# Diagonal score blocks in strips of 64 queries, two groups in 17 chunks, one bound per branch

## The chip, the cores and the metric

The kernel runs on one core of one Trainium2 chip. The metric is the device time of one execution in microseconds; three runs of the kernel before gave 198.6 to 199.15 us, median 198.92 us.

## The reference

The input x has 1024 tokens of 256 numbers. It is layer-normed, goes through a causal attention with 16 heads and through a gated FFN, and both results are added to it.

```python
xn = layernorm(x)
q1, k1, q2, k2, v = split(xn @ Wqkv)          # 16 heads; q, k of 8 numbers each, v of 16
A1 = causal_softmax(q1 k1^T / sqrt(8)) v      # first branch
A2 = causal_softmax(q2 k2^T / sqrt(8)) v      # second branch
diff = (A1 - lam * A2) / rms * (1 - LAMBDA_INIT)
ffn = (gelu(fp8(xn) @ fp8(w_gating[0])) * (fp8(xn) @ fp8(w_gating[1]))) @ fp8(w_linear)
out = x + diff @ Wproj + ffn
```

## The kernel before

Tokens come in eight blocks (TB) of 128, P = 128. A group g is four heads (J) of one branch; there are eight groups, four (HG) for each branch, of which the first four are branch one. The queries and keys of a head lie in 32 rows of `q_st` and `k_st` (float32r, high and low parts stacked, so that a head's rows are 32j to 32j+31), the values in `v_all` (float32, 32 columns for a head: 16 values, a one in column 16, zeros behind).

Scores stand with keys on partitions and queries on columns. Of a group only blocks on or below the diagonal are made: 9 chunks of 512 columns per head, listed in `CHUNKS` (line 46) as (key block, blocks of queries, first query). Three of the nine have two pieces, (128, 384), (256, 256) and (128, 384) columns; eight 128-wide blocks on the diagonal are in five of them (`DIAGONALS`, line 51). A chunk of one head is an item and fills one PSUM bank; a unit is three items. A group is 36 items or 12 units (STEPS), the kernel 96 units (UNITS).

The main loop is `attention` (line 958). For each unit n TensorE runs
- `scores(n)` (line 877): it waits until exp n-2 is done (banks 0 to 2 and 3 to 5 take turns), then makes the pieces in rounds, the first piece of all three items, then the second. Each matmul has 32 rows of contraction, so the three heads sit in different row groups of the array. Its line in the profile is L898.
- `values_due(n)` (line 950): the probabilities of an earlier chunk times `v_all`, summed in bank 6; per piece one matmul for each of the four heads, in four column groups of 32 (`product`, line 906, profile line L910; float32, so each shows as two passes). They come 5 units after the chunk's last unit, 2 to 4 near the end (`due`, line 86).
- `beside(n)` (line 817): at hand-set units (V_AT, QK_AT, NORM_AT, DOWN_AT, lines 70 to 78) a part of the remaining projections of v, q and k (L758, L752), norms, or of the FFN's down product (L851). Some of these parts are split over two units.

ScalarE runs one exp of 1536 columns per unit (L442), from PSUM to one of six chunk slots of `probs`; its bias is a bound per group (`shift`, made by `bound`, line 454, once per branch). GpSimd zeroes the upper triangles of the diagonal blocks with one affine_select per chunk that has some (`mask`, line 356, L366), and has four squarings (L340) and four residual additions (L372) placed between masks. VectorE transposes each half of a group's sums out of bank 6 (`take`, L594), divides, subtracts the branches, normalizes and transposes back; it also takes the split projections and norms.

Ahead of the loop lie the input DMAs (x in four DMAs of two blocks: two on SyncE, L244, two on ScalarE, L385), the layer norm, transposes, first projections and the FFN's up product. Behind it lie the last output projections (`ending`, line 977) and five output DMAs (L312, L314, L452). Each output DMA holds 128 partitions, by whole blocks. On SP the output DMAs stand in one queue in the order of blocks 0-1, 2-3, 4-5, 7.

Of the kernel before, what the change touches and what calls it, by code (L numbers as in the profile page):

```python
# [15 lines left out]
P = 128  # L16
T = 1024
# [14 lines left out]
VW = 32  # L32
# [15 lines left out]
DIAGONALS = {0: [0], 1: [0, 128], 2: [0, 256], 4: [0], 6: [0, 128]}  # L48
NC = len(CHUNKS)
ITEMS = NC * J  # L50
PER_UNIT = 3
STEPS = ITEMS // PER_UNIT
UNITS = GROUPS * STEPS
BRANCH = HG * STEPS
KEPT = 6
STACKS = 4
MIXED, LAST = 2, 8
# [9 lines left out]
Y_BANK = (7, 7, 0, 0, 1, 2, 3, 4)  # L67
# [8 lines left out]
NORM_AT = {23: 0, 31: 1, 39: 2, 41: 3}  # L76
DOWN_AT = {44: (0, 0, 4), 45: (0, 4, 8), 49: (1, 0, 8), 56: (2, 0, 4), 57: (2, 4, 8), 61: (3, 0, 8), 65: (4, 0, 8),
           68: (5, 0, 4), 69: (5, 4, 8), 73: (6, 0, 8), 79: (7, 0, 4), 80: (7, 4, 8)}


def last_unit(chunk):

    return (chunk * J + J - 1) // PER_UNIT


def due(g, c):

    if g < GROUPS - 2:
        late = 5
    elif g < GROUPS - 1:  # L90
        late = 4
    else:
        late = (3, 3, 3, 3, 3, 2, 2, 2, 2)[c]
    return g * STEPS + last_unit(c) + late


def diagonals_until(g, c):

    return g * len(DIAGONALS) + sorted(DIAGONALS).index(c) + 1

# [19 lines left out]
def diff_attention_ffn_kernel(nc, x, w_qkv, w_proj, lq1, lk1, lq2, lk2, w_gating, w_linear, out):  # L120
    x_rows = x[0].rearrange("(b p) c -> p b c", p=P)
    out_rows = out[0].rearrange("(b p) c -> p b c", p=P)

    with ExitStack() as ctx:
# [31 lines left out]
        max_rest = arena[0:HG * J, 3 * T:5 * T].rearrange("p (a t) -> p a t", a=2)  # L156
        max_junk = arena[:, 5 * T:6 * T].bitcast(BF16).rearrange("p (a t) -> p a t", a=2)
# [6 lines left out]
        w_q = sb("w_q", [P, KC, 3 * C], F32)  # L164
        causal = sb("causal", [P, T], BF16)

        o_t = sb("o_t", [P, 2, 16, VW], F32)
        attn1 = sb("attn1", [P, HG, 32, DV], F32)

        squares = sb("squares", [P, 4, T], BF16)  # L170
# [868 lines left out]
```

## Time and profile before

| | us | |
|---|---|---|
| median of three runs | 198.92 | 198.6 to 199.15 |
| the profiled execution | 199.27 | its span 197.5 |
| TensorE matmul busy | 182.2 | 92% of the span |
| ScalarE busy | 163.6 | 83% |
| VectorE busy | 92.4 | 47% |
| GpSimd busy | 59.4 | 30% |
| mean granted TensorE clock | 0.993 | |

The span runs from the first to the last instruction; 1.8 us of the profiled execution lie outside it. Matmuls overlap in the array, so that the busy time of TensorE counts a stretch as busy when any matmul is in flight. The chain of waits is the sequence of work, followed back from the last instruction, in which each piece was what the next one waited for or ran behind. Its pieces for one stretch, listed in order of time, lie end to end, so the length of a piece is what it costs on that path.

### The profile page before, as it was taken

To read this page: it belongs to the slowest core of one execution; us is meant where nothing else is said; L and a number is where in the kernel's file an instruction comes from. 1 tells how busy PE (TensorE), PEld (TensorE's weight loads), DVE (VectorE), ACT (ScalarE), POOL (GpSimd) and SP (SyncE) were. 2 spreads that over 40 slices of the span, in tenths; PEclk is the share of its full clock that TensorE was granted. 3 is DMA by queue.
4 is the path that set the end of the run, shared out by engine and by line. 5 is a ranking of instruction groups with operands and counts; after the bars stand their busy time and mean duration, and the time that the engine had idled before them with its cause. 6 is when DMAs were issued, how large, how long until landed. Compare 5 with 4: busy or idle time off the path is not lost.

```text
span 197.5 us, 3554 instructions
## 1 busy us (share of the span) xinstructions
PE 182.2 (92%) x1446; PEld 78.3 (40%) x1450; DVE 92.4 (47%) x218; ACT 163.6 (83%) x136; POOL 59.4 (30%) x71
## 2 busy tenths in 40 slices
PE   6899989899999999999989999999998999899940
PEld 6855334454332323242333424344342423233830
DVE  0975798431223240540472025216703697895840
ACT  2156865899999999999999999999999899998010
POOL 8526600042216142314442043235216124320000
PEclk9999999999999999999999999999999999999997
DMA  5967377780000000000277781000000000000051
GB/s 174 404 242 245 73 179 205 207 190 10 0 0 3 0 0 3 0 0 3 60 203 188 181 191 39 0 3 0 0 3 0 0 3 0 0 3 0 0 178 44
DMA packets 8149, 14.99 MB, mean 76 GB/s; under 512 B 1984, under 2 KB 5312, under 8 KB 8128
## 3 DMA queue, kind: packets, MB, share of 16 engines
q1 hardware_dynamic: 7440, 14.05, 25.5%
q10 hardware_dynamic: 688, 0.66, 1.0%
q8 instruction: 14, 0.23, 0.5%
q14 instruction: 7, 0.06, 0.1%
HBM read 5.26 MB, written 1.05 MB: 32 GB/s over the span
## 4 chain that ended last, share of the span: by engine, by line
PE 74%; ACT 15%; DVE 4%; POOL 1%; issue 1%; POOLq 0%; DVEq 0%
PE ps L910 29%; PE ps L898 17%; ACT probs L442 13%; PE ps L752 8%; PE ps L758 4%; PE ps L941 4%; PE ps L747 3%; PE ps L851 3%; PE ps L813 3%; DVE area L529 2%; DVE o_t L594 1%; ACT probs L430 1%; PE ps L742 1%; PE ps L947 1%; ACT L430 1%
## 5 line engine op out<-in xcount | busy, mean ns | idle before, releaser
L442 ACT ACTIVATE probs<-ps,shift 128x1536 f32<-128x1536 f32 x96 | 140.1, 1554 | 2.4 <-PE ps L898 1.6
L910 PE MATMUL ps<-probs,v_all 128*32 128x512 f32 (+3 forms) x768 | 78.1, 496 | 1.5 <-DVE o_t L594 1.5
L366 POOL TENSOR_SCALAR_AFFINE_SELECT probs<-probs 128x1024 f32<-128x1024 f32 (+1 forms) x40 | 36.7, 917 | 109.7 <-ACT probs L442 109.6
L898 PE MATMUL ps<-q_st,k_st 32*128 32x512 f32 (+3 forms) x384 | 49.8, 420 | 1.2 <-issue 0.8
L898 PEld LDWEIGHTS ps<-q_st,k_st 32*128 32x128 f32 x384 | 22.4, 182 | 58.6 <-ACT probs L442 30.4
L594 DVE STREAM_TRANSPOSE o_t<-ps 128x512 f32<-128x512 f32 x16 | 11.5, 717 | 49.5 <-PE ps L910 49.5
L910 PEld LDWEIGHTS ps<-probs,v_all 128*32 128x32 f32 x768 | 16.4, 108 | 19.6 <-issue 13.9
L752 PE MATMUL ps<-xn_t,w_q 128*128 128x512 f32 (+1 forms) x38 | 17.3, 557 | 0.8 <-ACT xn_t L393 0.8
L813 PE MATMUL ps<-area 128*128 128x512 fp8e4 x64 | 14.5, 379 | 1.0 <-DVE area L529 1.0
L430 ACT ACTIVATE probs<-ps 128x512 bf16<-128x512 f32 x16 | 9.3, 597 | 4.5 <-PE ps L813 2.7
L529 DVE TENSOR_TENSOR area<-ps,probs 128x512 fp8e4<-128x512 f32 x16 | 10.5, 687 | 1.8 <-ACT probs L430 1.7
L813 PEld LDWEIGHTS ps<-area 128*128 128x128 fp8e4 x64 | 6.0, 97 | 9.5 <-issue 3.4
L758 PE MATMUL ps<-w_q,xn_t 128*128 128x256 f32 x32 | 8.7, 399 | 1.0 <-DVE area L529 1.0
L650 DVE CAST parts<-ps 128x512 fp32r<-128x512 f32 x4 | 2.8, 691 | 14.2 <-PE ps L752 14.1
L752 PEld LDWEIGHTS ps<-xn_t,w_q 128*128 128x128 f32 x38 | 6.2, 189 | 7.3 <-issue 7.0
L851 PE MATMUL ps<-area 128*128 128x256 fp8e4 x64 | 9.1, 275 | 0.0
L941 PE MATMUL ps<-w_p,squares 128*128 128x256 f32 x32 | 8.4, 389 | 0.0
L747 PE MATMUL ps<-ident 128*128 128x128 f32 x36 | 6.8, 378 | 1.6 <-POOL ident L321 1.6
L747 PEld LDWEIGHTS ps<-ident 128*128 128x128 f32 x36 | 6.6, 290 | 1.6 <-POOL ident L321 1.6
L496 DVE TENSOR_TENSOR parts<-ps,parts 128x512 fp32r<-128x512 f32 x8 | 5.5, 690 | 3.5 <-ACT parts L399 3.4
L851 PEld LDWEIGHTS ps<-area 128*128 128x128 fp8e4 x64 | 5.3, 97 | 4.6 <-issue 4.1
L941 PEld LDWEIGHTS ps<-w_p,squares 128*128 128x128 f32 x32 | 5.8, 190 | 2.6 <-issue 1.9
(78 smaller groups left out, 117.2 us busy)
## 6 DMA issues: line engine op xcount, KB each, us to landing
q_st<-parts SPq DMA_DIRECT2D x32, 128.0 KB, 2.8
k_st<-parts SPq DMA_DIRECT2D x32, 128.0 KB, 2.8
probs<-L_ffn_w_gating SPq DMA_DIRECT2D x4, 512.0 KB, 7.8
probs<-L_ffn_w_linear SPq DMA_DIRECT2D x1, 1024.0 KB, 13.1
w_q<-L_attn_Wqkv SPq DMA_DIRECT2D x2, 384.0 KB, 5.8
out<-probs SPq DMA_DIRECT2D x3, 256.0 KB, 3.0
x_sb<-L_attn_x SPq DMA_DIRECT2D x2, 256.0 KB, 4.2
x_sb<-L_attn_x ACTq DMA_DIRECT2D x2, 256.0 KB, 4.5
```

The costliest lines, as they stand in the source:

```text
L366: pool.affine_select(out=blocks, in_=blocks, pattern=pattern, compare_op=ALU.is_ge, fill=0.0, base=0, channel_multiplier=-1).then_inc(mask ...
L442: act.activation(probs[:, at:at + PER_UNIT, :].rearrange("p s u -> p (s u)"), ps[:, 3 * (n % 2):3 * (n % 2) + 3, :].rearrange("p b n -> p ...
L529: dve.tensor_tensor(hidden[:, c, h * HALF:(h + 1) * HALF], ps[:, 2 * PAIR[n] + 1, :], gated[:, n % RING, :], ALU.mult, saturate=False).the ...
L594: dve.transpose(o_t[:, h, :, :].rearrange("p b w -> p (b w)"), ps[:, 6, :]).then_inc(o_taken, 1)
L747: pe.matmul(ps[:, 7, 0:P], ident[:, :], ident[:, :], start=True, stop=True)
L752: return pe.matmul(ps[:, bank, at:at + wide], w_q[:, k, i * P:(i + 1) * P], xn_t[:, k, h * HALF + at:h * HALF + at + wide], start=(k == 0 ...
L758: ins = pe.matmul(ps[:, bank, (b % 2) * C:(b % 2 + 1) * C], xn_t[:, k, b * P:(b + 1) * P], w_q[:, k, 2 * C:3 * C], start=(k == 0), stop=(k ...
L813: ins = pe.matmul(ps[:, 2 * PAIR[n] + g, :], w_gate8[:, g, k, c * P:(c + 1) * P], x8[:, k, h * HALF:(h + 1) * HALF], start=(k == 0), stop= ...
L851: ins = pe.matmul(ps[:, 7, (b % 2) * C:(b % 2 + 1) * C], hidden[:, c, b * P:(b + 1) * P], w_lin8[:, c, :], start=(c == 0), stop=(c == HC - 1))
L898: ins = pe.matmul(ps[:, bank, at:at + wide * P], k_st[rows, g % STACKS, kb * P:(kb + 1) * P], q_st[rows, g % STACKS, queries], start=True, ...
L910: ins = pe.matmul(ps[32 * j:32 * j + 32, 6, q0 % HALF:q0 % HALF + wide * P], v_all[:, g % HG, kb, 32 * j:32 * j + 32], probs[:, slot + j, ...
L941: ins = pe.matmul(ps[:, Y_BANK[b], at:at + C], out_t[:, p, b * P:(b + 1) * P], w_p[:, p, :], start=(p == 0 and at == 0), stop=(p == 1), sk ...
```

## The change

- The two diagonal blocks of an even and the next odd key block (a and a+1) are made in 192 columns instead of 256. Halves of blocks change places: in every odd block the lower and the upper 64 tokens are exchanged. A strip of 64 queries then needs all 128 keys of its own block, or 64 keys of each of two blocks, stacked on the 128 partitions. For that `v_all` gets a second copy (EARLY) that holds zeros where the other block's keys lie.
- Four of 17 chunks of a pair of groups hold such diagonals: eight pieces of 64 columns and one of 128 each. Two pieces of four write a strip of the same 64 columns, the second of them over 64 partitions only, so that eight pieces cover 384 columns.
- Two groups share 17 chunks (before 2 times 9). The kernel has 272 items in 92 units: 89 of three items, two of two and one of one, the odd ones at the middle and the end (STARTS).
- Per chunk with diagonals there are two affine_selects of 64 partitions and 1024 elements; 16 such chunks in all.
- One bound per branch instead of one per group serves as bias of the exps.
- `v_all` has 17 columns per head (VW), not 32; VectorE makes the EARLY copies with four copies.
- Parts of `beside` that were split over two units are whole, and all of them have new units; squarings and residual additions have new places; the delay of the values (LATER) is 5 units, 6, 4, 3 or 2 for some chunks.
- Every DMA of x and of the output that had 128 partitions becomes two of 64 partitions.

```diff
+def diagonal(at, a, c):
+    b, d = a + 1, c + 1
+    return [(at, b, FULL, b * P, MINOR), (at + 64, d, FULL, d * P, MINOR),
+            (at + 128, b, EARLY, b * P + MINOR, MINOR), (at + 128, a, EARLY, a * P, MINOR),
+            (at + 192, d, EARLY, d * P + MINOR, MINOR), (at + 192, c, EARLY, c * P, MINOR),
+            (at + 256, a, FULL, a * P + MINOR, MINOR), (at + 320, c, FULL, c * P + MINOR, MINOR)]
 CHUNKS = [
-    [(0, 4, 0)], [(3, 1, 384), (1, 3, 128)], [(2, 2, 256), (6, 2, 768)], [(0, 4, 512)], [(4, 4, 512)],
-    [(1, 4, 512)], [(7, 1, 896), (5, 3, 640)], [(2, 4, 512)], [(3, 4, 512)],
+    [(0, 0, diagonal(0, 0, 2) + [(384, 2, FULL, 384, 128)])],
+    [(0, 0, [(0, 0, FULL, 128, 384), (384, 1, FULL, 256, 128)])],
+    [(0, 0, [(0, 1, FULL, 384, 128)]), (0, 1, [(128, 4, FULL, 640, 384)])],
...
 ]
+MASKED = (0, 7, 9, 11)
+STARTS = list(range(0, ITEMS // 2, 3)) + [ITEMS // 2] + list(range(ITEMS // 2 + 2, ITEMS, 3)) + [ITEMS]
-QK_AT = {8: (4, 0, 0, 256), 9: (4, 0, 256, 256), 13: (4, 1, 0, 512), 17: (5, 0, 0, 512), 20: (5, 1, 0, 256),
-         21: (5, 1, 256, 256), 25: (6, 0, 0, 512), 29: (6, 1, 0, 512), 32: (7, 0, 0, 256), 33: (7, 0, 256, 256),
-         37: (7, 1, 0, 512)}
+QK_AT = {8: (4, 0, 0, 512), 13: (4, 1, 0, 512), 21: (5, 0, 0, 512), 25: (5, 1, 0, 512), 29: (6, 0, 0, 512),
+         32: (6, 1, 0, 512), 37: (7, 0, 0, 512), 39: (7, 1, 0, 512)}
+NORM_AT = {17: 0, 28: 1, 35: 2, 42: 3}
+DOWN_AT = {47: (0, 0, 8), 50: (1, 0, 8), 54: (2, 0, 8), 58: (3, 0, 8), 62: (4, 0, 8), 66: (5, 0, 8), 70: (6, 0, 8),
+           74: (7, 0, 8)}
+LATER = {20: 6, 26: 6, **{k: 4 for k in range(57, 63)}, 63: 3, 64: 3, 65: 3, 66: 2, 67: 2}
...
-            for b in (0, 4):
-                sp.dma_start(x_sb[:, b:b + 2, :], x_rows[:, b:b + 2, :]).then_inc(x_in[b // 2], 16)
+            for i in (0, 2):
+                for p0, rows in halves:
+                    sp.dma_start(x_sb[p0:p0 + MINOR, 2 * i:2 * i + 2, :], x_rows[:, i, rows, :]).then_inc(x_in[i], 16)
...
+            def mask(k):
+                at = k % KEPT * J
+                pool.wait_ge(exp_done, last_unit(k) + 1)
+                for p0, first in ((0, 0), (MINOR, P)):
+                    strips = probs[p0:p0 + MINOR, at:at + J, first:first + 4 * MINOR].rearrange(
+                        "p j (s u) -> p j s u", s=4)
+                    pool.affine_select(out=strips, in_=strips, pattern=[[0, J], [0, 4], [1, MINOR]],
+                                       compare_op=ALU.is_ge, fill=0.0, base=0, channel_multiplier=-1
+                                       ).then_inc(masked, 1)
+                    pool.wait_ge(masked, masks_until(k) - (p0 == 0))
...
-                for p in range(2):
+                for p in range(max(len(h) for h in heads)):
+                    for h in heads:
+                        if p < len(h):
+                            ins = score(*h[p], general)
...
+            def score(g, j, bank, piece, general):
+                at, kb, part, q0, wide = piece
+                rows, queries = slice(32 * j, 32 * j + 32), slice(q0, q0 + wide)
+                keys = MINOR if part == EARLY and kb % 2 == 0 else P
+                out = ps[0:keys, bank, at:at + wide]
+                ins = pe.matmul(out, k_st[rows, g % STACKS, kb * P:kb * P + keys], q_st[rows, g % STACKS, queries],
+                                start=True, stop=not general)
...
+                for at, kb, of, q0, wide in pieces:
+                    for j in range(J):
+                        ins = pe.matmul(ps[32 * j:32 * j + VW, 6, q0 % HALF:q0 % HALF + wide],
+                                        v_all[:, of, g % HG, kb, VW * j:VW * j + VW], probs[:, slot + j, at:at + wide],
+                                        start=first, stop=False, skip_group_check=True)
+                    first = False
```

## Rows read from the trace of the kernel before

**Rows 1.** The page's busy time, share of the span and instructions of each engine.

```profile
PE 182.2 (92%) x1446; PEld 78.3 (40%) x1450; DVE 92.4 (47%) x218; ACT 163.6 (83%) x136; POOL 59.4 (30%) x71
```

**Rows 2.** Groups by line: busy us, mean ns of one, idle before.

```profile
L442 ACT ACTIVATE probs<-ps,shift 128x1536 f32<-128x1536 f32 x96 | 140.1, 1554 | 2.4 <-PE ps L898 1.6
L430 ACT ACTIVATE probs<-ps 128x512 bf16<-128x512 f32 x16 | 9.3, 597 | 4.5 <-PE ps L813 2.7 <-DVE area L529 1.8
L366 POOL TENSOR_SCALAR_AFFINE_SELECT probs<-probs 128x1024 f32<-128x1024 f32 (+1 forms) x40 | 36.7, 917 | 109.7 <-ACT probs L442 109.6
```

**Rows 3.** The chain of waits from 45 to 60 us: start, length, what.

```profile
45.02 1.06 PE ps L758 x4
46.08 0.43 PE ps L898 x2
46.50 1.00 PE ps L910 x8
47.50 0.43 PE ps L898 x2
47.93 1.00 PE ps L910 x16
48.93 0.48 PE ps L898 x5
49.41 0.57 PE ps L910 x8
49.98 0.63 PE ps L752 x2
50.61 0.48 PE ps L898 x3
51.09 0.57 PE ps L910 x8
51.66 0.63 PE ps L752 x2
...
56.58 0.48 PE ps L898 x4
57.06 1.05 PE ps L752 x2
```

**Rows 4.** The chain of waits from 117 to 131 us.

```profile
117.92 0.99 PE ps L910 x8
118.91 0.43 PE ps L898 x2
...
121.40 0.54 PE ps L851 x4
...
128.30 0.98 PE ps L851 x8
```

**Rows 5.** ScalarE's instructions from 120 to 139 us: start, length, what.

```profile
118.68 21.58 ACT L442 ACTIVATE probs<-ps,shift 128x1536 f32<-128x1536 f32 x15
```

**Rows 6.** TensorE's matmuls, then its weight loads, from 83.4 to 87.4 us.

```profile
83.49 0.50 PE L898 MATMUL ps<-q_st,k_st 32*128 32x512 f32 x3
83.93 1.07 PE L910 MATMUL ps<-probs,v_all 128*32 128x128 f32 x16
85.25 0.55 PE L898 MATMUL ps<-q_st,k_st 32*128 32x128 f32 x6 [0.25 <-issue]
85.73 0.64 PE L910 MATMUL ps<-probs,v_all 128*32 128x256 f32 x8
...
85.25 0.30 PEld L898 LDWEIGHTS ps<-q_st,k_st 32*128 32x128 f32 x6 [0.23 <-issue]
```

**Rows 7.** Weight loads of the two lines: duration ns least, median, most.

```profile
L898 PEld LDWEIGHTS ps<-q_st,k_st x384: 180/181/186, 35.9 to 178.4; 32*128 32x128 f32 x192
L910 PEld LDWEIGHTS ps<-probs,v_all x768: 105/109/111, 46.4 to 181.8; 128*32 128x32 f32 x192
```

**Rows 8.** The chain of waits from 1 to 21 us.

```profile
8.40 0.89 PE ps L742 x8
```

**Rows 9.** The start: queues and VectorE, start, length, what, idle before.

```profile
0.80 0.95 SPq L244 DMA_DIRECT2D x_sb<-L_attn_x  x2
4.53 1.41 DVE L475 BATCH_NORM_STATS2 stats<-x_sb 128x6 f32<-128x256 f32 x4 [4.53 <-DMA x_sb<-L_attn_x]
```

**Rows 10.** The end: SyncE's queue from 188 us on.

```profile
188.34 2.73 SPq L312 DMA_DIRECT2D out<-probs  x3
191.11 0.50 SPq L314 DMA_DIRECT2D out<-probs  x1
```

**Rows 11.** Who waited for whom: us in total, times, longest.

```profile
PEld ps L910 <- POOL probs L366: 2.2, 7, 0.8
PEld ps L910 <- DVE o_t L594: 2.1, 8, 0.8
```

More of the change, by code:

```diff
@@ L65, with unit_of, last_unit, due @@
 WARM_UP = 18
-Y_BANK = (7, 7, 0, 0, 1, 2, 3, 4)
+Y_BANK = (7, 7, 5, 5, 0, 1, 2, 3)
 V_AT = {0: (2,), 1: (3,), 2: (4,), 3: (5,), 4: (6,), 5: (7,)}
-QK_AT = {8: (4, 0, 0, 256), 9: (4, 0, 256, 256), 13: (4, 1, 0, 512), 17: (5, 0, 0, 512), 20: (5, 1, 0, 256),
-         21: (5, 1, 256, 256), 25: (6, 0, 0, 512), 29: (6, 1, 0, 512), 32: (7, 0, 0, 256), 33: (7, 0, 256, 256),
-         37: (7, 1, 0, 512)}
[L76 to L99, printed above, removed]
+QK_AT = {8: (4, 0, 0, 512), 13: (4, 1, 0, 512), 21: (5, 0, 0, 512), 25: (5, 1, 0, 512), 29: (6, 0, 0, 512),
[4 more added lines that the diff above has]
+LATER = {20: 6, 26: 6, **{k: 4 for k in range(57, 63)}, 63: 3, 64: 3, 65: 3, 66: 2, 67: 2}
+def unit_of(item):
+    return max(n for n in range(UNITS) if STARTS[n] <= item)
+def last_unit(k):
+    return unit_of(k * J + J - 1)
+def due(k):
+    return last_unit(k) + LATER.get(k, 5)
+def ends(g):
+    return last_unit(g // 2 * NC + (8, 16)[g % 2])
+def begins(g):
+    return unit_of((g // 2 * NC + (0, 8)[g % 2]) * J)
+def masks_until(k):
+    return 2 * (k // NC * len(MASKED) + MASKED.index(k % NC) + 1)
 class Own:
@@ L672, in _ @@
             keep(0, 1)
+            norm_round(0)
             keep(1, 0)
             split(5)
-            norm_round(0)
             keep(1, 1)
-            split(6)
             norm_round(1)
             keep(2, 0)
+            split(6)
+            norm_round(2)
+            take(2, 1)
             split(7)
-            norm_round(2)
-            keep(2, 1)
+            divide(2, 1)
+            take(3, 0)
             norm_round(3)
@@ L931, in second_half @@
-            def second_half(g):
-                first, (kb, wide, q0) = CHUNKS[MIXED]
-                pe.wait_ge(o_taken, 2 * g + 1)
-                product(g, MIXED, first[1] * P, kb, wide, q0, True)
+                heads = []
+                for e, item in enumerate(range(STARTS[n], STARTS[n + 1])):
+                    k, j = item // J, item % J
+                    heads.append([(2 * (k // NC) + gi, j, 3 * (n % 2) + e, piece)
+                                  for gi, _, pieces in CHUNKS[k % NC] for piece in pieces])
@@ new lines, in values @@
+            def values(k, part):
+                c, slot = k % NC, k % KEPT * J
+                gi, h, pieces = CHUNKS[c][part]
+                g = 2 * (k // NC) + gi
+                if c in MASKED:
+                    pe.wait_ge(masked, masks_until(k))
+                else:
+                    pe.wait_ge(exp_done, last_unit(k) + 1)
+                if k == 0:
+                    pe.wait_ge(v_ones, 1)
+                    pe.wait_ge(zeros_set, 1)
+                    pe.wait_ge(v_out, 6)
+                    pe.wait_ge(early_out, 2)
+                if k == 2 and part == 1:
+                    pe.wait_ge(v_out, TB)
+                if k == 7:
+                    pe.wait_ge(early_out, 4)
+                first = (c, part) in OPENS
+                if first and (g, h) != (0, 0):
+                    pe.wait_ge(o_taken, 2 * g + h)
+                for at, kb, of, q0, wide in pieces:
[4 more added lines that the diff above has]
+                    first = False
+                if (c, part) in CLOSES:
+                    ins.then_inc(o_ready, 1)
@@ L950, in values_due @@
             def values_due(n, first, end):
-                for g in range(first, end):
-                    for c in range(NC):
-                        if due(g, c) == n:
-                            values(g, c)
-                        if c == MIXED and due(g, c) + 1 == n:
-                            second_half(g)
+                for k in range(first, end):
+                    for part in range(len(CHUNKS[k % NC])):
+                        if due(k) + part == n:
+                            values(k, part)
             def attention(br, general):
```

231 lines of the change are left out of this document (112 added, 119 removed).

## The prediction

> **What bounds the kernel now.** I read the busy times first [rows 1]: TensorE 92%, ScalarE 83%, the others under half. That names two candidates and decides nothing, because matmuls in flight side by side make TensorE look busy. So I took the chain of waits for stretches of the main loop [rows 3, 4]. There the pieces lie end to end and all of them are TensorE's: one unit's scores last 0.43 us, the values of a chunk 0.99 to 1.00, a projection part 1.05, and the next scores start as the piece before ends. The scores take the time of their 512 columns whether one head or three run beside each other in their row groups. So a unit with a chunk of values costs TensorE 0.43 + 1.00 = 1.43 us.
>
> Then ScalarE. Fifteen exps in a row begin 118.68 and end 21.58 later [rows 5]; less the last one's own length, some 1.6, this is 14 distances in 20 us, 1.42 to 1.43 us each. ScalarE's step and TensorE's step are the same to a hundredth, so either may be the bound. What decides is who gives way: ScalarE lost only 2.4 us in the whole loop [rows 2], but it cannot start an exp before its scores are there, and where TensorE has a dearer unit (0.48 for scores with a first piece of 128 columns, 0.57 + 0.63 beside them [rows 3], 1.68 together) the step of the kernel is 1.68, not 1.43. I take the loop as bound by TensorE, with ScalarE close behind. The reader should carry this away: an engine that is released from work gains nothing here if TensorE gets more.
>
> **The change part by part.** The sum is made against the profiled execution, 199.27 us; the median is 0.35 below it.
>
> Exps. 288 items of 512 columns become 272, that is 89 exps of 1536 columns, two of 1024, one of 512. At 1.43 for 1536, and by proportion for the rest, ScalarE needs 127.3 + 1.9 + 0.5 = 129.7 instead of 96 x 1.43 = 137.3 us: 7.6 less. This is off the path if TensorE is the bound, and counts zero.
>
> Units. Four units fewer. Each costs a round of scores, 0.43, and the switch back from values, which is 1.00 less the two passes of 0.43 = 0.14, of which I count 0.11. 4 x 0.54 = -2.2 us.
>
> Columns. Scores and values keep theirs. Chunks with diagonals have 8 x 64 + 128 = 640 columns on TensorE though only 512 for ScalarE, since two strips are written and read twice: a pair of groups has 4 x 640 + 13 x 512 = 9216, exactly the 18 x 512 of before. So TensorE is relieved of no stream; the saving is ScalarE's alone.
>
> Small score pieces, the largest term. A chunk with diagonals runs nine rounds, eight of 64 columns. A stream of 64 columns is 0.43/8 = 0.053 us, but each piece needs the weights of another key block in the same row group. Their spacing shows in the unit at 85.25 [rows 6]: six weight loads in two rounds last from 85.25 over 0.30 us, a single one 0.18 [rows 7], so the second round's load begins about 0.11 after the first. Transposes with 128 columns of weights and 128 of stream run at 0.89/8 = 0.11 [rows 8]. I therefore take 0.107 for a round with 128 keys and, by half its columns, 0.053 for the two rounds with 64. Eight distances: 6 x 0.107 + 2 x 0.053 = 0.75; first piece with its extra 0.05 (the 0.48 of a 128-column start less 0.43); last piece of 128 columns, 0.107. Together 0.91 against 0.43: +0.48 us. Four items never fit a unit of three, so each of the 16 chunks touches two units, and in a mixed unit the other heads' pieces end long before the nine rounds do: 32 units x 0.48 = +15.4 us. The lower bound is stream alone, 9 rounds in 0.53: +0.10 each, +3.3 us. The upper is the only distance from a short round to the next that the trace has: 0.48 less 384 columns at 0.32 is 0.16. 8 x 0.16 + 0.11 = 1.39, +0.96 each, +30.7 us. I choose 0.107, since loads were seen to follow each other at it.
>
> The units of before with a 128-column first piece, four per group, go: 32 x (0.48 - 0.43) = -1.6 us.
>
> Small value pieces. 16 chunks x 8 pieces x 2 passes = 256 passes of 64 columns. Two-piece chunks of before cost no more than single ones, 1.00 for sixteen matmuls against 1.00 for eight [rows 3], so a pass costs its stream and some nanoseconds: I take 3 ns, +0.8 us. Lower bound 0. The upper bound is one value weight load per pass, 0.109 [rows 7] instead of 0.053: +14 us. Seventeen instead of 32 columns of weights can only shorten the load; where it is hidden, this is nothing, and I count nothing.
>
> Joined parts. Three split projections, 2 x 0.63, become 1.05: -0.6. Four split down products, 2 x 0.54, become one of 0.98 [rows 4]: -0.4. Together -1.0 us.
>
> Masks. A mask of 1024 elements took about 1.1 (mean of both forms 0.92 [rows 2]); now two in a row for each chunk, 64 partitions each, with the same length: 2.3 us after the exp instead of 0.65 to 1.1. The total stays, 32 x 1.1 = 35 against 36.7. Values come five units after the chunk's last one; TensorE is at most two units ahead, so three steps, 4.3 us, cover 2.3, and also a residual of 1.2 ahead of it. With LATER 4 two steps, 2.9, cover 2.3 barely. Now the wait for masks is 2.2 us in total [rows 11], most of it hidden behind running matmuls. Zero, at most +2. What queues behind a late mask is TensorE's whole order.
>
> VectorE. Four more copies of some 0.5 us at a time when it is busy a quarter; shorter bound by one small reduction; zero. Its waits for TensorE around `take` remain; TensorE's waits for the transposes [rows 11] remain too, 16 halves as before.
>
> The odd units at the middle: ScalarE has 0.5 us of work where TensorE needs a whole round; TensorE does not wait for that. The flag of branch two comes from norms in unit 42 for unit 46, four steps, 5.7 us, for about 3 us of VectorE's work. Zero to +1.
>
> DMAs. An issue takes 0.5 us of a queue [rows 9, 10]. The first statistics wait for the first x, 4.53, and everything behind hangs on it; its second half is issued one place later: +0.4. w_q and the FFN's weights come 1 us later, which their users' 2 us of margin cover. At the end SyncE issues 8 instead of 4 DMAs, ScalarE 2 instead of 1; the last two wait for the same block, and the queue is full already (2.73 us for three). +0.5 at least, +1.7 if all of the queue's doubling shows; I take 1.0. Together +1.4 us.
>
> **Sum:** -2.2 + 15.4 - 1.6 + 0.8 - 1.0 + 1.4 = +12.8, so 199.27 + 12.8 = 212.1 us, 211.7 against the median; I say 212.
>
> **A rule of the pages.** The distance of 0.107 us for 128 columns of weights is what the trace gives in two places. The Trainium skill, "TensorE: Matmul & The Clock Gate", section "LDWEIGHTS (loading the stationary operand)", puts a load at its columns over 1.2 in ns, 107 for 128 and 53 for 64, whatever the rows; by that rule the sum stays as it is, and the trace agrees. It stands here because it denies the cheap case below: row groups don't make a load shorter.
>
> **The rivals.**
>
> *Small rounds cost their stream only.* For it: loads of other row groups start some ns apart [rows 6]. Against it: the 0.48 of a short first piece. The 15.4 becomes 3.3: 200.0 us.
>
> *ScalarE is the bound and the kernel gets faster.* The price of a diagonal unit would have to lie within what ScalarE's step leaves. Mixed units could hide the rounds beside other heads' 512 columns, and late scores be caught up by the two sets of banks. Then exps give -7.6, the DMAs +1.4: 193.1 us. For it: the steps are equal, 1.43, and ScalarE is never idle for long. Against it: in the chain of the loop nearly everything is TensorE, without a gap. It decides from an added TensorE time, small score and value pieces together, of under 2.2 + 1.6 + 1.0 - 1.4 = 3.4 us, which is 0.1 us per diagonal unit; above that the kernel is slower.
>
> *Every small round costs the long distance, or the array is emptied between tile shapes.* Rounds with 64 keys use another width of tile than those with 128, four changes in nine rounds. A change of shape is in the trace from values to scores, 0.11 to 0.14 us. Four of these per diagonal unit are +0.44 to 0.56, 32 x 0.5 = +16: 228 us. All rounds at 0.16 instead give +15.3 on the sum: 227.4 us. For it: 0.16 is the measured distance. Against it: the switch from scores to values costs nothing visible (0.43 for the scores before it). The Trainium skill, "TensorEngine Tiling (Array Packing)", section "Key Properties", says that changing the tiling mode drains the engine; by that rule this rival is the one that comes, and the 0.14 of the trace agrees in one direction of the two.
>
> *Every small value pass costs a whole weight load:* +13 on the sum, 225 us.
>
> **How the numbers follow.** Forecast, 207 to 218: 0.50. Cheap rounds, 198.5 to 206: 0.16. Long distance or emptied array, alone or in part, over 218 (224 to 229 in full): 0.18. Whole loads for value passes: 0.07. Faster, ScalarE bound: 0.09. The range takes the cheap rounds' 200 below and 228 above: 200 to 228. About 0.3% is what a measurement can tell from no change. Slower by over 0.3% hold the forecast, both dear cases and most of the cheap one: 0.87. Within 0.3%: 0.04, a part of the cheap case. Faster: 0.09.
>
> **What the new profile would show.** Scores of a unit with diagonals as chain pieces of about 0.9 us, eighteen or more matmuls each; 0.55 means the cheap case, 1.4 the dear one. Values of such a chunk about 1.05 to 1.1; 1.9 would be the load per pass. ScalarE with idle time ahead of exps, released by the scores, some 20 us in all, where it had 2.4; its step 1.43 in stretches without diagonals. TensorE's chain share up. First statistics at 4.9 to 5.0, and some 10 DMA issues at the end. What would make it wrong: exps still at 1.43 through the diagonal chunks, or TensorE waiting for masks for more than 2 us.

## The result and the profile after

Four runs of the changed kernel gave 223.03 to 229.54 us, median 224.8, beside 199.03 (198.6 to 199.22) for the kernel before: ratio 1.127, 95% interval 1.122 to 1.132. It is slower, and by about twice what the 212 of the prediction said. The profiled execution took 224.58 us (span 222.9) at a mean granted clock of 0.968, where before had 199.27 (197.5) at 0.993. Times and clock go together in the four runs (0.972 for the shortest, 0.952 for the longest); runs that the granted clock disturbed as a whole are left out of the ratios here and below.

First the page's busy times and the largest groups (columns as in [rows 1, 2]):

```profile
PE 202.4 (91%) x2879; PEld 113.3 (51%) x2884; DVE 97.4 (44%) x220; ACT 159.4 (72%) x132; POOL 60.0 (27%) x66
L505 ACT ACTIVATE probs<-ps,shift 128x1536 f32<-128x1536 f32 (+1 forms) x92 | 135.8, 1522 | 28.5 <-PE ps L979 27.8
L421 POOL TENSOR_SCALAR_AFFINE_SELECT probs<-probs 64x1024 f32<-64x1024 f32 x32 | 37.2, 1163 | 109.1 <-ACT probs L505 108.0
```

ScalarE's exps take 4.3 us less than in [rows 2], as the change wants, and ScalarE is idle ahead of them for 28.5 us where it was for 2.4; nearly all of that ended with scores (L979). TensorE has twice the instructions. The masks take as long in all as before, and no wait of TensorE for them is left. The shares of the chain of waits in the whole span, before and then after, show whose path grew:

```profile
PE 74%; ACT 15%; DVE 4%; POOL 1%; issue 1%; POOLq 0%; DVEq 0%
PE 72%; DVE 11%; DMA 4%; ACT 3%; issue 3%; SPq 2%; another core or an unknown queue 0%; DVEq 0%
```

The 15% of ScalarE before are in good part exps of the loop, 25.0 us, which the stretches of [rows 3, 4] do not hold. One piece of them:

```profile
110.07 7.30 ACT probs L442 x5
```

After the change nearly all of them are off the chain, and VectorE (DVE) stands there with 11% in place of 4%.

The chain of waits from 45 to 60 us, the same stretch as [rows 3]:

```profile
48.40 0.43 PE ps L979 x2
48.83 1.24 PE ps L1009 x72
...
55.13 1.04 PE ps L979 x20
56.17 0.98 PE ps L1009 x8
57.16 0.44 PE ps L979 x6
57.59 0.98 PE ps L1009 x8
58.58 1.04 PE ps L979 x27
```

Scores with nine rounds take 1.04 us whether all three heads have them (27 matmuls) or only some (20), against 0.43 for plain ones. The values of a chunk with diagonals (72 matmuls) take 1.24, of a plain one 0.98.

Start and end:

```profile
6.83 1.41 DVE L537 BATCH_NORM_STATS2 stats<-x_sb 128x6 f32<-128x256 f32 x4 [6.83 <-DMA x_sb<-L_attn_x]
213.36 5.81 SPq L362 DMA_DIRECT2D out<-probs  x6
219.22 1.80 SPq L365 DMA_DIRECT2D out<-probs  x2
```

Statistics start at 6.83 instead of 4.53 [rows 9]; eight output DMAs of 64 partitions hold SyncE's queue for 7.6 us, where four took 3.2 [rows 10]. From VectorE's last addition to the end of the span it is 7.5 us instead of 7.2.

The middle, in the chain from 108 to 132 us:

```profile
109.37 1.07 PE ps L827 x2
...
110.47 0.70 DVE parts L720
...
111.19 0.70 DVE parts L558
...
111.97 0.50 SPq L312
...
112.51 0.59 SPq L314
...
116.36 3.19 DMA k_st<-parts
...
119.60 1.62 PE ps L979 x18
121.22 1.84 PE ps L1009 x8
123.06 1.89 PE ps L979 x11
```

The last projection part (L827) is followed by VectorE's split, seven stacking DMAs issued one after another, and the landing of the last; the first scores of the second branch wait for it. Then the same pieces that took 1.04 and 0.98 take 1.9 and 1.84. The stretches of 5 us show why:

```profile
core 0: us, PE busy (x) PEld busy (x) DVE busy (x) ACT busy (x) POOL busy (x), PEclk, DMA share, GB/s
115.00:120.00 5.00, 3.82 (x107) 2.40 (x106) 2.71 (x13) 3.87 (x4) 0.00 (x0) 1.00 0.74 189
120.00:125.00 5.00, 5.00 (x48) 3.08 (x49) 0.00 (x0) 1.12 (x2) 0.00 (x0) 0.50 0.68 161
125.00:130.00 5.00, 5.00 (x26) 1.73 (x27) 0.00 (x0) 2.15 (x2) 2.30 (x2) 0.50 0.81 203
130.00:135.00 5.00, 4.59 (x64) 2.23 (x60) 1.40 (x3) 4.61 (x4) 0.00 (x0) 0.97 0.89 189
```

TensorE was idle for 1.2 of the 5 us before 120; from there it was granted 1.2 instead of 2.4 GHz for 10.2 us, which is 5.1 us of full speed.

**Where 25.3 us come from.** Ahead of the loop +1.7: the first exp begins at 39.73 instead of 38.01. In the loop, from the first exp to the start of the last, +22.2: 163.1 instead of 140.9. Behind it +1.4: 1.1 of that is one part of the output projection, which now stands behind the last exp and stood ahead of it, and 0.3 is the tail with the DMAs.

For the loop I count pieces at their price in the chain. Scores: before 96 x 0.43 + 32 x 0.05 = 42.9, after 32 x 1.04 + 60 x 0.43 = 59.1: +16.2. Values: before 72 x 0.995 = 71.6, after 16 x 1.24 + 52 x 0.98 = 70.8: -0.8. The half clock +5.1. TensorE's idle time in the loop is 7.75 us where it was 3.31, +4.4; in it are the wait for `k_st`, 0.9, and the waits for VectorE's transposes (`o_t`), 3.7 instead of 1.5. Joined parts by their lengths -1.0, and the projection part that left the loop -1.1. That is 22.8 where 22.2 were measured. It is a count times a price, not a sum of rows: in the chain of the kernel before, 25.0 of the loop's 140.9 us are exps, so that each term is known less well than the total suggests.

### The profile page after: what moved, and what is told of

The parts are those of the page before. It is cut to its first block, busy times and chain, and to the rows that moved or that the text cites. A ratio compares the mean times of both kernels' runs of the same rounds, so it can differ in the third digit from the quotient of the medians.

```text
span 222.9 us, 6456 instructions
## 1 busy us (share of the span) xinstructions
PE 202.4 (91%) x2879; PEld 113.3 (51%) x2884; DVE 97.4 (44%) x220; ACT 159.4 (72%) x132; POOL 60.0 (27%) x66
## 3 DMA queue, kind: packets, MB, share of 16 engines
HBM read 5.26 MB, written 1.05 MB: 28 GB/s over the span
## 4 chain that ended last, share of the span: by engine, by line
PE 72%; DVE 11%; DMA 4%; ACT 3%; issue 3%; SPq 2%; another core or an unknown queue 0%; DVEq 0%
PE ps L1009 27%; PE ps L979 23%; PE ps L827 7%; PE ps L833 4%; PE ps L922 3%; PE ps L1020 3%; PE ps L888 3%; DMA x_sb<-L_attn_x 2%; DVE o_t L656 2%; DVE area L591 2%; DMA k_st<-parts 1%; PE ps L817 1%; SPq L312 1%; ACT probs L493 1%; SPq L314 1%
## 5 line engine op out<-in xcount | busy, mean ns | idle before, releaser
L505 ACT ACTIVATE probs<-ps,shift 128x1536 f32<-128x1536 f32 (+1 forms) x92 | 135.8, 1522 | 28.5 <-PE ps L979 27.8
L1009 PE MATMUL ps<-probs,v_all 128*17 128x64 f32 (+4 forms) x1728 | 79.3, 315 | 4.2 <-DVE o_t L656 3.7
L979 PEld LDWEIGHTS ps<-q_st,k_st 32*128 32x128 f32 (+1 forms) x864 | 46.3, 182 | 48.6 <-issue 35.3
L979 PE MATMUL ps<-q_st,k_st 32*128 32x64 f32 (+5 forms) x864 | 67.6, 317 | 2.4 <-issue 1.0
L421 POOL TENSOR_SCALAR_AFFINE_SELECT probs<-probs 64x1024 f32<-64x1024 f32 x32 | 37.2, 1163 | 109.1 <-ACT probs L505 108.0
L1009 PEld LDWEIGHTS ps<-probs,v_all 128*17 128x17 f32 x1728 | 27.6, 97 | 21.2 <-issue 13.7
L827 PE MATMUL ps<-xn_t,w_q 128*128 128x512 f32 x32 | 16.4, 621 | 1.2 <-ACT xn_t L456 0.8
L888 PEld LDWEIGHTS ps<-area 128*128 128x128 fp8e4 x64 | 6.0, 97 | 9.3 <-issue 3.2
L827 PEld LDWEIGHTS ps<-xn_t,w_q 128*128 128x128 f32 x32 | 5.3, 189 | 6.2 <-issue 4.9
L922 PEld LDWEIGHTS ps<-area 128*128 128x128 fp8e4 x64 | 5.9, 103 | 4.6 <-issue 2.4
L392 POOL TENSOR_TENSOR squares<-parts 128x512 bf16<-128x512 f32 x4 | 4.2, 1042 | 12.8 <-DVE parts L720 12.2
```

Source lines behind the costliest of these rows:

```text
L421: pool.affine_select(out=strips, in_=strips, pattern=[[0, J], [0, 4], [1, MINOR]], compare_op=ALU.is_ge, fill=0.0, base=0, channel_multipl ...
L505: act.activation(probs[:, at:at + many, :].rearrange("p s u -> p (s u)"), ps[:, 3 * (n % 2):3 * (n % 2) + many, :].rearrange("p b n -> p ( ...
L827: return pe.matmul(ps[:, bank, at:at + wide], w_q[:, k, i * P:(i + 1) * P], xn_t[:, k, h * HALF + at:h * HALF + at + wide], start=(k == 0 ...
L888: ins = pe.matmul(ps[:, 2 * PAIR[n] + g, :], w_gate8[:, g, k, c * P:(c + 1) * P], x8[:, k, h * HALF:(h + 1) * HALF], start=(k == 0), stop= ...
L922: ins = pe.matmul(ps[:, 7, (b % 2) * C:(b % 2 + 1) * C], hidden[:, c, b * P:(b + 1) * P], w_lin8[:, c, :], start=(c == 0), stop=(c == HC - 1))
L979: ins = pe.matmul(out, k_st[rows, g % STACKS, kb * P:kb * P + keys], q_st[rows, g % STACKS, queries], start=True, stop=not general)
```

## The experiments

### The DMAs alone

```diff
-                sp.dma_start(x_sb[:, b:b + 2, :], x_rows[:, b:b + 2, :]).then_inc(x_in[b // 2], 16)
+                for p0 in (0, 64):
+                    sp.dma_start(x_sb[p0:p0 + 64, b:b + 2, :], x_rows[p0:p0 + 64, b:b + 2, :]).then_inc(x_in[b // 2], 16)
```

(the same for ScalarE's two, and for the five of the output)

> The kernel before, with each DMA of x and of the output as two of 64 partitions and nothing else. In the changed kernel a half DMA holds its queue for 0.6 to 0.8 us and the first statistics begin at 6.83 instead of 4.53 us, the first exp at 39.73 instead of 38.01, and from the last exp to the end it takes 20.0 instead of 18.6 us. Theory: all of that is the DMAs', so 199.0 + 1.7 + 1.5 = 202.2 us. Rival, as forecast: half a place in the queue at each end, 199.0 + 1.4 = 200.4 us.

Measured: 202.3 us, ratio 1.014 (1.010 to 1.018) to the kernel before. In SyncE's queue at the end:

```profile
191.26 4.74 SPq L314 DMA_DIRECT2D out<-probs  x6
196.05 2.97 SPq L317 DMA_DIRECT2D out<-probs  x2
```

A row's mean misleads here, since three of the rows hold one long issue each: 1.60 us in the row of three of [rows 10], 1.30 and 2.33 in these two. The others take 0.60 to 0.70 for 64 partitions and 0.42 to 0.50 for 128. At the start four take 2.99 in both kernels with halves, 0.75 each against 0.48 [rows 9]. So a half is dearer to issue than a whole.

The 2.9 us are not all of that, though. In the profiled run the first exp comes 2.9 us later than before, and 1.7 of these are the clock:

```profile
10.00:15.00 5.00, 4.22 (x9) 1.88 (x8) 3.98 (x15) 1.39 (x4) 0.00 (x0) 0.66 0.99 375
```

The first projections, 3.67 us in the kernel before and in the changed one, take 5.37 here. TensorE had waited 1.8 and 0.8 us ahead of them. Without the clock the halves cost 1.2 at the start and 0.4 behind the last exp, 1.6 in all; the run of the four with the highest mean clock, 0.990, took 201.15, 1.8 above before. Then the lower halves of x went on SyncE's queue and the upper ones on ScalarE's:

```diff
-            for b in (0, 4):
-                for p0 in (0, 64):
-                    sp.dma_start(x_sb[p0:p0 + 64, ...
+            for b in (0, 2, 4, 6):
+                sp.dma_start(x_sb[0:64, b:b + 2, :], x_rows[0:64, b:b + 2, :]).then_inc(x_in[b // 2], 16)
```

> e1, with the lower halves of x on SyncE's queue and the upper ones on ScalarE's, so that both halves of the first two blocks are first in their queues. Theory: e1's loss at the start is the second half's place behind a first of 0.75 us; the first exp comes some 1.2 us earlier than in e1 and the time is 202.3 - 1.2 = 201.1 us. Rival: half DMAs are slower in themselves, 202.3 us.

Measured: 200.65 us, ratio 1.0075 (1.0045 to 1.0105). 2.9 us above before have become 1.5. The order in the queue does what was expected for the first statistics, which start at 4.00 us (before 4.53, with the halves in one queue 6.05). But the profiled run (203.1 us) has its first exp at 40.89, no earlier than that kernel's 40.87: its first projections wait for `w_q` until 11.15, whose issues now stand behind four of x, and then take 5.40 at half clock. The faster runs have a mean clock of 0.988 to 0.990. How much of the 1.4 us is order and how much is clock is not shown.

### The small score pieces

Here the diagonal chunks' scores are made in two pieces of 384 and 128 columns; the exchange of halves is not computed, so part of the scores is left out.

```diff
-                                  for gi, _, pieces in CHUNKS[k % NC] for piece in pieces])
+                                  for gi, _, pieces in CHUNKS[k % NC] for piece in one_piece(k % NC, pieces)])
```

> The changed kernel, where the eight small score pieces of a diagonal chunk are one of 384 columns with one key block; the scores are not those of the reference. Theory: a unit with diagonals takes 0.44 instead of 1.04 us on TensorE and all of it is on the path: 224.8 - 32 x 0.60 = 205.6 us. Rival: TensorE's rounds are partly hidden and ScalarE or the half clock takes over, under half of it comes back: over 215 us.

Measured: 209.9 us, ratio 1.051 (1.048 to 1.055): 14.9 less than the changed kernel, the largest single part. The chain shows 0.43 where 1.04 was, that is 32 x 0.61 = 19.5 less; some 4 of it came back as a wait, of value matmuls for VectorE's transposes of the sums (who waited for whom, TensorE):

```profile
PE ps L1016 <- DVE o_t L663: 7.8, 10, 3.4
```

In the changed kernel the same row says 3.7 us, 7 times. The next kernel keeps the nine rounds and gives each of the eight small ones 64 keys (half of the keys of six rounds is left out):

```diff
-                keys = MINOR if part == EARLY and kb % 2 == 0 else P
+                keys = MINOR if wide == MINOR else P
```

> The changed kernel, where all eight small score pieces load 64 keys instead of six with 128 and two with 64, so that half of each block's keys is left out. The streams are unchanged. Theory: the columns of the weight load pace a round, 0.111 us for 128 and 0.057 for 64: six rounds 0.054 shorter, a unit with diagonals 0.72 instead of 1.04 us, 224.8 - 32 x 0.32 = 214.5 us. Rival, tile shapes that differ cost a drain and loads cost nothing: rounds of one shape save only the four changes, and those took nothing in the trace, so 224.8 us.

Measured: 213.86 us, ratio 1.078 (1.071 to 1.085): 10.9 less. The unit with 27 matmuls, first in the changed kernel, then here (timeline, weight loads: start, length):

```profile
58.51 0.97 PEld L979 LDWEIGHTS ps<-q_st,k_st 32*128 32x128 f32 x27 [0.85 <-ACT probs L505]
```

```profile
56.99 0.65 PEld L979 LDWEIGHTS ps<-q_st,k_st 32*64 32x64 f32 x27 [0.85 <-ACT probs L505]
57.06 0.72 PE ps L979 x27
```

Columns streamed and the number of matmuls are the same, only the key columns of six rounds are halved, and the loads shrink by 0.32. The first row less a single load's 0.18 [rows 7] is 0.79 for eight distances, six with 128 keys and two with 64. One by one, the loads of a round begin 0.109 to 0.112 us behind those of the round before if that had 128 keys, and 0.059 if it had 64 (0.055 to 0.059 in the second kernel). Six times 0.053 less is the 0.32. The spacing of rounds is the weight load. It also denies the emptied array: the changed kernel has four changes between 64 and 128 keys in a unit, this one only that to the last piece, and there is nothing left over for changes beyond those six halves. The rule of the Trainium skill, "TensorEngine Tiling (Array Packing)", section "Key Properties", that a change of the tiling mode drains the engine, finds no cost at this change of width.

The total fits less well than it seems: 10.9 measured for 32 x 0.32 = 10.2, but the profiled run of this kernel has no half clock in the loop, where the changed kernel lost 5.1, so that the agreement of the totals is in part chance.

Last, two pieces of an odd block made by one matmul that streams 128 columns into both strips, with the projections placed earlier (as in the experiments on the middle, below).

```diff
+                if wide == BOTH:
+                    out = ps[:, bank, 0:4 * MINOR].rearrange("p (s e u) -> p s e u", s=2, e=2)[:, :, at // MINOR, :]
```

> e2, with the two score pieces of each odd block made by one matmul of 128 columns into two strips: seven rounds instead of nine, result unchanged. Theory: two loads of 128 columns fewer per unit with diagonals, 32 x 0.22 = 7.0 us under e2's 221.6: 214.6 us. Rival: the streams are what counts, and those are the same: 221.6 us.

Measured: 212.95 us, ratio 1.070 (1.068 to 1.073). Two rounds fewer per unit give 0.82 in place of 1.04:

```profile
58.10 0.82 PE ps L996 x19
```

32 x 0.22 = 7.0, and 8.6 were gained on the kernel that it was made from, whose profiled run lost 1.7 in the loop to half clock where this one lost nothing; 7.0 + 1.7 is 8.7. Still 14 us short of the kernel before.

### The small value pieces

```diff
-                for at, kb, of, q0, wide in pieces:
+                for at, kb, of, q0, wide in one_piece(c, pieces):
```

Part of the values' sums is left out by this.

> The changed kernel, where the eight small value pieces of a diagonal chunk are one of 384 columns with one set of values; the sums are not those of the reference. Theory: a diagonal chunk's values take 0.98 instead of 1.24 us: 224.8 - 16 x 0.26 = 220.6 us. Rival: the rest of the chain hides them, 224 us or more.

Measured: 222.63 us, ratio 1.114 (1.107 to 1.120), 2.2 less. Its runs spread over 4 us and the changed kernel's over 6.5, so the direction fits and the size stays open; the 1.24 and 0.98 of the chain are the better number: 16 x 0.26 = 4.2 for the diagonal chunks.

### The middle: the late split

Projection parts, squares, splits and norms are moved ahead, the last projection from unit 39 to 32, and VectorE's order with them.

```diff
-QK_AT = {8: (4, 0, 0, 512), 13: (4, 1, 0, 512), 21: (5, 0, 0, 512), 25: (5, 1, 0, 512), 29: (6, 0, 0, 512),
-         32: (6, 1, 0, 512), 37: (7, 0, 0, 512), 39: (7, 1, 0, 512)}
+QK_AT = {8: (4, 0, 0, 512), 11: (4, 1, 0, 512), 18: (5, 0, 0, 512), 20: (5, 1, 0, 512), 24: (6, 0, 0, 512),
+         26: (6, 1, 0, 512), 30: (7, 0, 0, 512), 32: (7, 1, 0, 512)}
```

> The changed kernel, with the eight split projections and four norms in units 8 to 35 instead of 8 to 42, squarings and VectorE's order to match, so that the q and k of the second branch are stacked well before unit 46. Theory: the late last split (unit 39) held SyncE's stacking DMAs, so that TensorE waited 1 us for k_st at unit 46 and then ran at half clock from 119.6 to 129 us, which cost 4.7 more: 224.8 - 5.7 = 219.1 us, with the clock at 1.00 throughout. Rival: the clock falls because small rounds keep little of the array busy, whatever the wait: only the 1 us goes, 223.8 us.

Measured: 221.59 us, ratio 1.108 (1.101 to 1.114), 3.2 less, not 5.7. The wait for `k_st` is gone, but the clock fell again at the change of branch, for a shorter time:

```profile
120.00:125.00 5.00, 5.00 (x40) 2.04 (x37) 0.00 (x0) 2.02 (x2) 2.30 (x2) 0.66 0.57 144
```

0.66 over 5 us is 3.4 us at half. In the 8 us ahead of it TensorE had waited 0.57 and 0.33 us, nothing longer. Then only the last two parts were moved, and their split put ahead of one transposition of VectorE:

```diff
-         32: (6, 1, 0, 512), 37: (7, 0, 0, 512), 39: (7, 1, 0, 512)}
+         32: (6, 1, 0, 512), 36: (7, 0, 0, 512), 37: (7, 1, 0, 512)}
...
+            split(7)
             take(2, 1)
-            split(7)
```

> The changed kernel with one difference: the two parts of the last q and k projection stand at units 36 and 37 instead of 37 and 39, and VectorE splits them before it takes the second half of group 2. The stacking DMAs then start some 4 us earlier. Theory (the wait for k_st at the start of the second branch is what lets the granted clock fall to half for 10.2 us there): no wait for k_st, no fall at this place: 1.0 + 5.1 = 6 us less than the changed kernel, 218 to 220. Rival A (the clock falls at the change of branch anyway, at another wait, as it did in the kernel with all parts earlier, for some 3.4 us): 1.0 + 3.4 less, 220 to 222. Rival B (the fall has nothing to do with the wait): 223.5 to 224.5.

Measured: median 223.5 us, ratio 1.1125 (1.107 to 1.119). Its runs differ: two took 220.07 and 220.57 at a clock of 0.994 and 0.993, the latter being the profiled one, whose clock is whole in all of the loop:

```profile
118.00:123.00 5.00, 4.67 (x60) 2.53 (x56) 0.21 (x1) 3.37 (x4) 0.00 (x0) 1.00 0.56 157
123.00:128.00 5.00, 4.83 (x54) 2.25 (x51) 0.00 (x0) 4.13 (x4) 2.30 (x2) 1.00 0.76 184
```

The others took 222.87 to 227.4 at 0.982 to 0.957. So the clock can stay up without the wait for `k_st`, and the profiled run is then 4.0 us below that of the change, where wait and half clock together were put at 6.1; TensorE waits 1.1 us longer for `ffn` there (1.9 instead of 0.8 us). By the median the gain is 1.3 us, so the theory's 218 to 220 is missed.

Nor is the wait enough for the fall. The kernel with 64 keys in each small piece waits for `k_st` just as long, at 113.6 us, and its clock stays up to the end of the loop (the wait; the granted clock in 40 slices of the span):

```profile
PE ps L979 <- DMA k_st<-parts: 0.9, 1, 0.9
PEclk9999999999999999999999999999999999999995
```

In the change the clock fell after 0.94 us of this wait and in the kernel with one value piece after 1.68, both times for 10.2 us; with one score piece it fell after 1.13, for 3.4 us. The wait of 1.9 for `ffn` above was followed by none. The wait is an occasion on which the clock fell in some kernels; what decides is not shown.

### Everything small taken out

Scores and values of diagonal chunks each in two pieces, projections earlier; the same parts left out as in the two kernels above.

> The changed kernel with the earlier splits of e2, and with scores and values of diagonal chunks each in one piece of 384 columns; the result is not the reference's. It keeps the 92 exps, the masks, the odd units and the half DMAs. Asked: is ScalarE's saving worth anything once TensorE is no dearer. Theory: e2's 221.6 less e3's 14.9 less e4's 2.2 is 204.5 us, since what is saved in rounds is in part given back in waits for bank 6 to be emptied; no gain over before. Rival, ScalarE as the bound: 199.3 - 7.6 + 2.9 (the DMAs, e1) = 194.6 us.

Measured: 206.18 us, ratio 1.036 (1.034 to 1.038). ScalarE has its fewer exps and TensorE no small piece, and still it is 7 us slower than before. ScalarE is idle 17.1 us ahead of exps. The profiled run of 208.67 us, the slowest of five, has its worst stretch here (columns as above):

```profile
170.00:175.00 5.00, 1.99 (x15) 0.63 (x19) 4.79 (x9) 1.97 (x3) 2.97 (x3) 0.76 0.00 0
175.00:180.00 5.00, 4.73 (x38) 1.31 (x34) 1.24 (x5) 3.38 (x3) 0.00 (x0) 0.50 0.00 0
180.00:185.00 5.00, 5.00 (x38) 1.57 (x32) 4.45 (x17) 2.63 (x2) 0.00 (x0) 0.50 0.00 0
185.00:190.00 5.00, 5.00 (x37) 1.51 (x34) 1.51 (x3) 3.94 (x3) 0.00 (x0) 0.88 0.02 3
```

TensorE waits 3.5 us for VectorE (its row for `o_t` has 7.5 us in all), and the half clock after it costs more than the wait: 1.2 + 2.5 + 2.5 + 0.6 = 6.8 us. From 160 to 173 us the chain is VectorE's: it divides, normalizes and squares before it takes the sums out of bank 6. In the chain of this loop, 148.5 us, 32.3 are exps and 22.3 VectorE's. So ScalarE's saving did not come out in this kernel; what it would be worth with VectorE's order mended and the clock up, no run shows.

### Single terms on the kernel before

The 384 columns first and the 128 last, so that no unit begins with a short round:

```diff
-    [(0, 4, 0)], [(3, 1, 384), (1, 3, 128)], [(2, 2, 256), (6, 2, 768)], [(0, 4, 512)], [(4, 4, 512)],
-    [(1, 4, 512)], [(7, 1, 896), (5, 3, 640)], [(2, 4, 512)], [(3, 4, 512)],
+    [(0, 4, 0)], [(1, 3, 128), (3, 1, 384)], [(2, 2, 256), (6, 2, 768)], [(0, 4, 512)], [(4, 4, 512)],
+    [(1, 4, 512)], [(5, 3, 640), (7, 1, 896)], [(2, 4, 512)], [(3, 4, 512)],
```

> The kernel before with one difference: in chunks 1 and 6 the piece of 384 columns is made first and the piece of 128 last, so that the first round of a unit is never a round of 128 columns; the two diagonal blocks of such a chunk then stand in columns 0 and 384 and get one affine_select each (8 chunks of a branch pair with two selects of 512 elements instead of one of 1024). Theory (TensorE binds the loop, and ScalarE follows): the scores of some 32 units take 0.43 instead of 0.48 us on the chain, 32 x 0.05 = 1.6 us less: 197.4 to 197.8. Rival (ScalarE's own step of 1.43 us binds, and the 0.05 are hidden): 199.1 to 199.3. Second rival (GpSimd's additional selects delay the values): above 199.5.

Measured: 197.7 us, ratio 0.9937 (0.992 to 0.9954): faster by the 1.6 us of TensorE's chain less a little. So TensorE bound most of the loop of before. ScalarE is close: exps make up 58.0 of the 139.5 us of this loop's chain, where they were 25.0. And with 17 columns for the values (in the products' slices too):

```diff
-VW = 32
+VW = DV + 1
```

> The previous kernel, with 17 columns of v_all per head in the value products instead of 32, and nothing else of the change. The plain passes of values measured 0.98 us in the changed kernel beside 0.99 to 1.00 before: 80 chunks x 0.01 to 0.02 us = 0.8 to 1.6 us less where TensorE binds: 196.2 to 197.0, if the previous kernel gives 197.6. Rival (ScalarE's step binds by then, or the narrow load brings nothing): within 0.3 us of the previous kernel.

Measured: 196.89 us, ratio 0.9887 (0.9868 to 0.9907), 0.8 more. This is the best kernel of the study. The chain around a projection in two halves:

```profile
48.58 0.43 PE ps L902 x6
49.02 0.56 PE ps L914 x8
49.57 0.63 PE ps L756 x2
50.20 0.42 PE ps L902 x3
50.62 0.57 PE ps L914 x8
51.19 0.63 PE ps L756 x2
```

Then the joined parts:

```diff
-QK_AT = {8: (4, 0, 0, 256), 9: (4, 0, 256, 256), 13: (4, 1, 0, 512), 17: (5, 0, 0, 512), 20: (5, 1, 0, 256),
-         21: (5, 1, 256, 256), 25: (6, 0, 0, 512), ...
+QK_AT = {9: (4, 0, 0, 512), 13: (4, 1, 0, 512), 17: (5, 0, 0, 512), 21: (5, 1, 0, 512), 25: (6, 0, 0, 512), ...
```

> The kernel with the wide piece first and 17 columns of v_all, and in addition the joined parts of the change: the three q and k parts of 256 columns twice become one of 512, at units 9, 21 and 33, and the four down products of four steps twice become one of eight, at units 45, 57, 69 and 80. Theory (this term of the sum is -1.0 on TensorE's path): 195.7 to 196.2. Rival (ScalarE's banks cannot cover a unit of 0.43 + 1.0 + 1.05, so that ScalarE waits there for what the joining saves, or ScalarE's step binds): 196.6 to 197.3.

Measured: 199.41 us, ratio 1.0012 (0.9999 to 1.0025): 2.5 slower than the kernel with halves, where the term says 1.0 faster.

```profile
66.81 0.43 PE ps L901 x6
67.25 0.60 PE ps L913 x8
...
67.94 0.73 DVE o_t L597
68.67 0.04 issue
68.72 0.63 PE ps L913 x8
69.34 1.05 PE ps L755 x2
```

Between the two halves of a group's values VectorE transposes bank 6 (0.73). The first half of the projection stood in exactly this gap. Joined and put behind, it leaves TensorE with a round of scores alone to do. The pair of units takes 3.59 us (66.81 to 70.40) against 3.24 (48.58 to 51.82), +0.35; were it so in all seven places, 2.5. Seen in the waits, TensorE for `o_t`: 4.2 us, 9 times, here; 1.5 us, 3 times, with halves, so six new waits and +2.7.

## Why the prediction was right or wrong

**What held and what was luck.** The direction held. The forecast's own band, 207 to 218, did not: 224.8 lies in the band that the prediction gave to the long distance and the emptied array (0.18), and the stated range of 200 to 228 holds it because these rivals stretched it upward. Their mechanism did not come. The sum was +12.8 and the measured change is about twice that.

**The bound was right in the main.** Taking 0.05 us from 32 units of TensorE shortened the kernel by 1.35, and ScalarE's saving could nowhere be seen. But "in the chain of the loop nearly everything is TensorE" was read from two stretches; over the whole loop 25.0 of 140.9 us are exps.

**The largest term had the right mechanism and was too small.** A unit with diagonals was put at 0.91 and is 1.04, 32 x 0.13 = 4.2 us more. The eight distances were nearly right (0.79 in the loads, 0.75 forecast; the 0.107 that I took was a little below the 0.11 that the rows gave). What was sized too low is the rest: 1.04 - 0.79 = 0.25, where I had 0.16 for the first piece and the last. The mixed units did cost as much as whole ones (x20 and x27 both 1.04).

**Four units fewer and the value pieces.** Forecast -2.2 and +0.8, together -1.4; by the chain the scores of four units give -1.7 and all values -0.8, together -2.5. The difference is in the main the 17 columns of weights, which I had counted at nothing and which gave 0.8 on the kernel before. My forecast of "about 1.05 to 1.1" for a diagonal chunk's values was wrong by my own count: 128 columns more in two passes are 0.21 us, so 1.24 had to be expected. The sum had it right, since four chunks fewer pay for it.

**A 128-column first piece less:** -1.6 forecast, -1.35 measured alone, with what the additional mask instructions cost in it.

**Masks** were put at zero, and TensorE's wait for them, 2.2 us before, is gone.

**Joined parts: the wrong sign.** I took 2 x 0.63 against 1.05 and did not ask what the first 0.63 covered. Alone, on the kernel with the wide piece first and 17 columns, this is +2.5 instead of -1.0. In the changed kernel, where the parts stand in other units, it's in between: TensorE's idle time for `o_t` is 3.7 us instead of 1.5, so that I put it at +1.2, an estimate from those rows and not shown by a run.

**VectorE was put at zero** and has a part in this: its share of the chain went from 4% to 11%, where I expected TensorE's share to rise. How much of the 2.2 us is due to its order and how much to the joined parts no run separates.

**DMAs: the size was near, the parts were not.** +1.4 forecast. In the changed kernel's trace the start is +1.7 and the tail +0.3; alone, with the clock taken out, 1.2 and 0.4. An issue of 64 partitions was taken at 0.5 us of a queue and holds it for 0.6 to 0.8. The first statistics came at 6.83, not 4.9 to 5.0. What I did not foresee is that TensorE, made to wait at the start, can run its first projections at half clock: 1.7 us more in the kernel with the DMAs alone, though not in the changed kernel. And the margin of 2 us for `w_q` did not hold with the halves of x on two queues, where TensorE waited for it in the profiled run.

**The middle was a step missed.** I followed the flag and the norms to unit 46 and gave them four steps. The other thing that unit 46 waits for is `k_st`, behind split 7 (now two units later), VectorE's order, and seven issues of SyncE at 0.6 us with a landing of 3.2. I named SyncE's queue for the x and output DMAs only. The wait is 1.0 us, and 5.1 us of clock stand behind it, so by the rows this is the largest miss, 6.1 us. With the wait away and the clock up, 4.0 us came back; and since the same wait passed without a fall in the kernel with 64 keys, the 5.1 belong to this kernel's executions and not to the wait as such.

**The rivals.** Cheap rounds: denied by 1.04. ScalarE bound and faster: not seen in any kernel with the changed units, 206.18 at best, though that one has VectorE's waits and half clock in it. The emptied array or 0.16 for every round: denied by 1.04 and by the kernel with 64 keys, although its 227 to 228 lies nearer to the measured time than my 212 does; the total alone would have taught the wrong cause. Whole loads for value passes: denied by 1.24.

The misses add: 4.2 for the diagonal unit less 1.1 for units and values, 0.6 for the DMAs, 2.2 for the joined parts and VectorE, 6.1 for the middle: 12.0, where 224.6 is 12.5 above 212.1. The agreement is better than the terms are known. How the remaining waits and falls of the clock divide between runs is open, since they differ from run to run.

## What to carry to other kernels

When an engine is full, ask of every piece of work that is moved or joined what it stood in front of: a half part of 0.63 us that looks like overhead can be the cover of another engine's 0.73. Saving columns with small tiles pays only if the number of weight loads in a row does not grow; here 128 keys in a load are worth 0.11 us whether they serve 64 columns or 128. And follow every semaphore that a stage's first unit waits for back through its queues, not only the one that the change is about.

## What the runs showed of the hardware

- Where the granted clock fell to half (1.2 GHz) in the loop it stayed there for 3.4 us (projections earlier, one score piece, one value piece), 10.2 us (the change, one value piece) or 13.7 us (no small pieces). Ahead of most falls TensorE had waited 0.9 to 3.5 us, but only 0.57 and 0.33 us with projections earlier, and 0.37 us before a fall of 3.4 at 42 us with one value piece; waits of 0.92 us (64 keys) and 1.9 us (last split earlier) were followed by no fall. No run of the kernel before had a mean below 0.987.
- At the start, waits of 1.8 and 0.8 us were followed by 3.4 us at half clock in the kernel with the DMAs alone, and the same eight matmuls of projection took 5.37 instead of 3.67 us; waits of 1.5 and 0.8 (64 keys) and of 1.2 and 0.8 (the change) were not.
- Issuing a DMA over 64 partitions held its queue for 0.54 to 0.83 us for the most part, one over 128 partitions for 0.37 to 0.50, at twice the bytes. Single issues of output DMAs took longer: 1.60 us over 128 partitions, 1.2 to 3.2 over 64.
- Score rounds whose heads stand in different row groups still follow each other at one load's spacing, 0.109 to 0.112 us for 128 columns of weights and 0.055 to 0.059 for 64, and a change between the two widths costs nothing that can be seen.
